# The causal mask of grouped attention, added by VectorE in PSUM instead of by three TensorE products per head

## The reference

```
q = q * cos + rotate_half(q) * sin          # 32 heads, 512 tokens, 128 wide
k = k * cos + rotate_half(k) * sin          # 8 heads, each used by 4 query heads
scores = q @ k.T / sqrt(128)
scores = scores * scale                     # keys 0..34 by 0.5, keys 35..106 by 1.5, for queries from 107 on
scores = scores + where(qpos >= kpos, 0, float32 min)
attn = softmax(scores) @ v
out = attn @ wo.T
```

## Time and profile before

| | |
|---|---|
| median of 3 runs | 3147.85 us (3145.69 to 3154.63) |
| the profiled execution, its own time | 3139.91 us |
| its span, first to last instruction | 3137.8 us |
| mean granted TensorE clock | 0.874 |
| busy in the whole span | PE 2461.8 us (78%), DVE 2008.0 (64%), ACT 1584.7 (51%), POOL 1127.0 (36%) |
| first and last mask product | 1760.9 and 2550.0 us |

### The profile page before, as it was taken

One profiled execution on the slowest core, in us unless ns is written; L12 is line 12 of the kernel. 1 busy time (PEld: TensorE's weight loads), 2 busy tenths in 40 slices (PEclk: granted clock), 3 DMA queues, 4 the chain that ended last, 5 costly groups with the idle time before them and its releaser, 6 DMA issues.

```text
span 3137.8 us, 36611 instructions
## 1 busy us (share of the span) xinstructions
PE 2461.8 (78%) x12408; PEld 1933.7 (62%) x12408; DVE 2008.0 (64%) x3083; ACT 1584.7 (51%) x3186; POOL 1127.0 (36%) x992
## 2 busy tenths in 40 slices
PE   6986989578688857868799799998999986951076
PEld 4344357467577746756678688876788864841065
DVE  4824744688677667867653567772677754398974
ACT  1632631465665256666520466662666641699511
POOL 2011046141122441112267456565465640300180
PEclk8886899689898968989999899999999997965588
DMA  6132122110200120010023111122111110100010
GB/s 212 42 97 80 42 78 81 48 38 4 64 21 24 44 71 21 18 51 21 28 70 110 43 44 45 48 58 61 31 53 48 52 41 14 54 14 0 0 48 27
DMA packets 85967, 152.56 MB, mean 49 GB/s; under 512 B 8632, under 2 KB 17464, under 8 KB 85656
## 3 DMA queue, kind: packets, MB, share of 16 engines
q1 hardware_dynamic: 85784, 150.24, 16.3%
HBM read 135.06 MB, written 14.75 MB: 48 GB/s over the span
## 4 chain that ended last, share of the span: by engine, by line
PE 37%; ACT 8%; DVE 5%; issue 4%; POOL 3%; POOLq 0%; ACTq 0%; DVEq 0%
PE ps L614 33%; ACT tables L1274 5%; PE ps L628 4%; POOL w_lo L558 1%; ACT m L1156 1%; ACT tables L1128 1%; POOL w_hi L557 1%; POOL k L571 1%; DVE stat L1328 1%; DVE n L1336 0%; DVE tables L1748 0%; DVE f_lo L1313 0%; DVE x_sb L1316 0%; DVE f_hi L1312 0%; ACT m L1138 0%
## 5 line engine op out<-in xcount | busy, mean ns | idle before, releaser
L557 POOL TENSOR_SCALAR w_hi<-w_in 128x512 fp32r<-128x512 f32 x418 | 315.1, 754 | 1453.3 <-PE ps L614 886.9
L558 POOL TENSOR_TENSOR w_lo<-w_in,w_hi 128x512 fp32r<-128x512 f32 x418 | 596.5, 1427 | 34.9
L614 PE MATMUL ps<-hT_hi,w_lo 128*128 128x512 f32 x864 | 353.8, 409 | 19.2 <-DVE a L1358 12.9
L1517 DVE TENSOR_TENSOR_SCAN m<-m,m 128x1028 f32<-128x1028 f32 x128 | 307.3, 2400 | 67.2 <-ACT m L1156 59.7
L628 PE MATMUL ps<-tables,m 128*128 128x128 f32 x1024 | 187.8, 313 | 202.5 <-ACT tables L1128 117.9
L614 PE MATMUL ps<-hT_hi,w_hi 128*128 128x512 f32 x864 | 341.7, 396 | 0.0
L614 PE MATMUL ps<-hT_lo,w_hi 128*128 128x512 f32 x864 | 341.7, 395 | 0.0
L614 PE MATMUL ps<-m,tables 128*128 128x128 f32 (+1 forms) x2112 | 323.1, 302 | 13.3 <-ACT tables L1128 12.6
L614 PEld LDWEIGHTS ps<-m,tables 128*128 128x128 f32 (+1 forms) x2112 | 293.2, 213 | 23.4 <-ACT tables L1128 17.2
L628 PEld LDWEIGHTS ps<-tables,m 128*128 128x128 f32 x1024 | 129.7, 158 | 238.3 <-ACT tables L1128 141.3
L1128 ACT ACTIVATE tables<-ps 128x512 f32<-128x512 f32 x256 | 151.0, 590 | 184.5 <-PE ps L628 183.0
(11 more groups left out here) (232 smaller groups left out, 5503.0 us busy)
## 6 DMA issues: line engine op xcount, KB each, us to landing
w_in<-units SPq DMA_DIRECT2D x418, 256.0 KB, 2.6
stack_scratch<-a SPq DMA_DIRECT2D x48, 256.0 KB
a<-stack_scratch SPq DMA_DIRECT2D x64, 192.0 KB, 4.5
m<-bc_scratch SPq DMA_DIRECT2D x16, 512.0 KB, 5.2
out<-x_sb SPq DMA_DIRECT2D x2, 1024.0 KB, 4.3
tables<-small SPq DMA_DIRECT2D x1, 1399.0 KB, 10.1
x_sb<-x SPq DMA_DIRECT2D x4, 256.0 KB, 3.5
x_sb<-x SPq DMA_DIRECT2D x1, 1024.0 KB, 7.2
```

The source lines that it names most:

```text
L557: c["did"](nc.gpsimd.tensor_scalar(w_hi[:, r], raw, 1.0, 1.0, ALU.mult, ALU.mult), s["unit_hi"])
L558: c["did"](nc.gpsimd.tensor_tensor(w_lo[:, r], raw, w_hi[:, r].bitcast(F32), ALU.subtract), s["unit_split"])
L614: ins = T.matmul(out, lhsT, rhs, start=start, stop=stop)
L1517: V.tensor_tensor_scan(states, m_dA[:, dA:dA + NG].rearrange("p a t -> p (a t)"), states, 0.0, ALU.mult, ALU.add)\
```

## The change

The float32r copies `ident_r` and `mask_r` and the two DVE instructions that made them are gone. The scores of row tiles 1 to 3 end with the third product of `mm3`, which now raises `g_scores`. A new DVE helper `hide(t)` adds the mask to the diagonal block of row tile t in place: it reads PSUM and the table in SBUF and writes PSUM. `maxima_1` calls it for tile 1, `maxima_2` for tiles 2 and 3 before their row maxima.

```
-        ident_r = sb("ident_r", [P, P], F32R)
-        mask_r = sb("mask_r", [P, P], F32R)
...
-                            mm3(o, q_hi, q_lo, g_k_hi[:, g, 0:w], g_k_lo[:, g, 0:w], True, False)
-
-                            mm(o[:, t * P:w], ident_r[:, :], mask_r[:, :], False, True, s["g_scores"])
+                            mm3(o, q_hi, q_lo, g_k_hi[:, g, 0:w], g_k_lo[:, g, 0:w], True, True, s["g_scores"])
...
-                        go(V.tensor_copy(ident_r[:, :], ident))
-                        go(V.tensor_copy(mask_r[:, :], col("mask")))
...
+                def hide(t):
+
+                    bank, at_s = g_bank[t]
+                    own_keys = ps[:, bank, at_s + t * P:at_s + (t + 1) * P]
+                    return V.tensor_tensor(own_keys, own_keys, col("mask"), ALU.add)
+
...
                 def maxima_1():
 
                     need(s["g_scores"])
+                    go(hide(1))
+                    did(V.tensor_tensor(g_s0, ps[:, 0, 0:P], col("key_scale"), ALU.mult))
                     go(top(1))
-                    did(V.tensor_tensor(g_s0, ps[:, 0, 0:P], col("key_scale"), ALU.mult))
                     did(V.tensor_tensor(g_s0, g_s0, col("mask"), ALU.add))
...
                     need(s["g_scores"])
+                    go(hide(2))
+                    need(s["g_scores"])
+                    did(hide(3))
                     go(top(2))
-                    need(s["g_scores"])
                     did(top(3))
```

More of the change, by code:

```diff
@@ L1358, in attn_qk @@
                         go(V.tensor_tensor(a_lo[:, qk], ps[:, 4 + qk], a_hi[:, qk].bitcast(F32), ALU.subtract), s["a_lo"])
-                    if b == 0 and m == 0:
-                        go(V.tensor_copy(ident_r[:, :], ident))
-                        go(V.tensor_copy(mask_r[:, :], col("mask")))
                     if b == 0 and m == 1:
```

## The result

| | before | change |
|---|---|---|
| median of 5 runs | 3145.69 us (3142.61 to 3154.63) | 3124.86 us (3116.91 to 3128.16) |
| ratio to before, 95% interval | | 0.9932 [0.9911, 0.9953] |
| the profiled execution, its own time | 3139.91 us | 3127.87 us |
| its span | 3137.8 us | 3126.0 us |

The change is faster, by 20.8 us between the medians. The two profiled executions differ by 12.0 us. Whole executions scatter by about as much as the change is worth, so what it does in its own stage is measured there: from one fixed product of PE to another, in the traces.

A forecast was written before the change was run, and what follows sets the result against it. PE was taken to bound the grouped attention. Per batch, -0.20 (head 0), +0.53 (head 1) and +8.41 (heads 2 to 31), doubled, gave 17.5 us off 3147.85: 3130.3 us; own range 3124 to 3136, 8 in 10 within 3122 to 3144.

The forecast's parts named there:

- The bound: Grouped attention: PE busy for all 46.86 us of a four-head group, so time off its list shortens the span.
- What leaves PE: Scores of each head: three mask products removed, worth 0.29 us per head by steps from start to start.
- The rival of the bare steps: Scores on PE: only the mask products' own steps go, 0.18 us per head, 3136.8 us; chance 0.12.
- the estimate of 15.6 us made from its 81 ns: PE's scores: 192 removed products priced at the skill page's sustained step of a 128-column product with weight load.
- What comes to DVE: `maxima_1` and `maxima_2`: three additions per head at 0.28 us each, making DVE 0.70 us later per head.
- The rival with additions as dear as L1611: DVE's additions each cost 0.29 us more, using up the room at the query split: 3133.2 us; chance 0.12.
- Is there room for it?: DVE's turn with `add(3)`: 4.48 us of work fits in 4.49; POOL's query split keeps 0.69 us to spare.
- The edges: Start and end of each batch: head 0 loses 0.20 us, head 1 gains 0.53, heads 2 to 31 gain 8.41.
- In the last head ... I charge nothing there: Last head of each batch: DVE's shifts lie ahead of ACT's copies of transposed tiles, so no loss is counted.
- DVE becomes the bound: Query split after a key split: DVE's lateness makes groups slower once additions pass 0.90 us each; chance 0.06.
- the gain is given back elsewhere: PE's wait moves to ACT's swap or the weight units; time stays within 0.3% of 3147.85 us; chance 0.06.

The follow-up runs named there:

- e2: Kernel before with the DVE mask additions put on top, PE's mask products kept: group of four heads 46.86 us, stage 1.8 us longer than before.
- e1: Changed kernel without the three DVE additions, row tiles 1 to 3 left unmasked: median 3130.09 us, stage 16.5 us shorter than before.
- e5: Changed kernel with row tile 0's scores kept in PSUM, so its mask addition has one SBUF input: median 3126.83 us.
- e6: Changed kernel with row tile 0 in PSUM and each mask addition covering two row tiles, two per head instead of four: median 3127.7 us.
- e3: Changed kernel with each of the three DVE additions made twice: median 3143.97 us, stage 3.6 us longer than before.
- e4: Changed kernel with the two float32r tiles of mask and identity still allocated and made once by DVE: ratio 0.9931 to the kernel before.
- e9: Changed kernel, unaltered, measured and profiled again on another chip: ratio 0.995 [0.9938, 0.9963] to the kernel before.

## Why the prediction was right, and where it was not

**The bound.** Right. PE was busy for all of 46.86 us and is busy for all of 45.71 (the forecast said 45.7), and e2 shows that DVE's additions alone leave the group at 46.86.

**What leaves PE.** Right at 0.29 us per head, and right in where it comes from. Set beside each other, the scores of one head before and in the change draw apart by 0.06 at each removed product and by another 0.05 to 0.06 at each of the two long steps of 0.23 and 0.29 that followed one (0.18 and 0.23 in their place); 0.24 ahead of the transposes stayed. The rival of the bare steps, 0.18 per head, would have made the group 46.14 us; the bank still changes at those places, so it was not the bank. That the weight load behind a short product is what made the steps long is a reading that no run tests. The page "TensorE: Matmul & The Clock Gate" ("Back-to-back issue gap") of the Trainium skill, by the estimate of 15.6 us made from its 81 ns, does not agree: the 26 distances per batch outside the edges shrank by 0.29 us each in the mean, 97 ns per removed product. (The 3132.3 us made from it also left out the edges' 0.4, which the rival of the bare steps counts.)

**What comes to DVE.** Right: 0.293 us per addition where 0.28 was taken. The unknown, a write into PSUM, cost 12 ns. The page "SBUF — State Buffer" ("Who interferes with whom") of the Trainium skill, by which one SBUF input does not contend with GpSimd, agrees: 192 additions with one SBUF input lasted 279 to 300 ns, also with PSUM as output, while L1611 with two reached 1417. The rival with additions as dear as L1611 falls.

**"Is there room for it?"** This step failed in size. It left 0.69 us to spare at the split of the query; 0.05 to 0.50 was measured, and 0.05 is none. The instructions I added were counted well (0.73 against 0.70), but three things around them were not. The 0.98 it started from was one turn's: the same kernel had 0.79 and 0.63 at two others. L1611 was taken at 0.29 from one row, though the rows' mean was 573 ns, and in its new place it was held for 0.30 more. And one of GpSimd's own instructions, L555 ahead of L556 and the split, lasts 1.14 to 1.15 us in every such turn, where it lasted 0.94 in most before:

```profile
1950.89 0.94 POOL L557 TENSOR_SCALAR w_hi<-w_in 128x512 fp32r<-128x512 f32 x1
```

The runs tell the last two apart. In e1, without the additions, L555 lasts 0.94 and the room is 0.71 to 0.73 in nine of the ten turns, close to the 0.69 forecast; in the tenth L555 lasts 1.14 and the room is 0.52. In e5, with the additions but without L1611's second SBUF input, L555 lasts 1.14 and the room is 0.49 to 0.51 everywhere. So the longer L555 takes 0.20, and L1611's holds take up to 0.45 more and make the spread. What lengthens L555 is a reading: DVE's L1544, which has two SBUF inputs, runs beside it in the change (from 1945.52, L555 from 1945.55). (The 3.78 us counted as work in the earlier trace rows also held 0.15 us of waiting for a transposed tile. It is gone in the change, but the instruction behind that copy starts 0.12 later, so the count came out.)

**The edges.** This is the term of the sum that was mis-sized. In the window from the first to the last scores the forecast is 17.2 us (17.5 less the last head), measured 13.6. By the differences from head to head, batch 0 and batch 1: head 28 was taken as unchanged and lost 0.45 and 0.46; head 30 was taken as a full gain and lost 0.45 and 0.45, 0.74 short each; head 2 gained nothing for 0.29; head 1 gained 0.31 and lost 0.16 for a forecast gain of 0.53, but that head differs by 0.75 between profiles of one kernel, so its share says nothing. Head 0 was taken 0.20 too dear: it stayed at 14.80. Together 3.5 of the 3.6. Less head 1 in both, the forecast is 16.1 and 13.5 was measured.

At head 28 VectorE's additions are the cause: without them (e1) it is 9.99, as before. At head 30 they are a part. Of the 0.74 short, leaving the additions out gives back 0.30 in batch 0 and 0.23 in batch 1 (e1, 8.91 in batch 0), taking L1611's second SBUF input away gives back 0.40 (e5, 8.81), and both remedies on VectorE together 0.47 (e6, 8.74). The last 0.27 came back in no run. In the trace of the change DVE goes from `add(3)` (2100.30) to that copy (2103.13) without a pause, and the scores begin only at 2100.39; so shorter scores on PE do not bring the copy forward. "In the last head ... I charge nothing there" held, but I did not look at the head before it, where PE's copy wait lay uncovered at 0.31 us already.

**DVE becomes the bound.** Not here, but nearer than forecast. The rival put the point at 0.90 us per addition; e3, where a doubled addition with its waits comes to about 0.5 (0.73 us per head as above, and about 0.8 for the second round, over three; 0.6 with the 0.26 by which the mask of tile 0 got longer), already gave the whole gain back. It did so for the most part through ACT's swap and scaling, which is the mechanism of the rival "the gain is given back elsewhere", and only for 0.10 of 0.77 through the query's split.

**The size of the whole.** 3124.86 us was measured where 3130.3 was forecast, 20.8 us less than before instead of 17.5, while the stage gave 13.9 with its last head. That the total came nearer to the forecast than the stage did is luck: e4 finds nothing outside the stage, e9 gave 17.0 us between the medians for the same kernel, and the start of the stage moves by 5 us and the stretch behind it by 3.5 us between profiles of the same kernel. 13.9 of 3143 us is a ratio of 0.9956; it lies within the second interval and just above the first's end of 0.9953. What makes whole executions scatter stays open beyond the granted clock of their first stages, and what decides that clock does too.

## What to carry to other kernels

Where one engine is busy for all of a repeated group, work taken from it is worth its step from start to start, including how it lengthens the next instruction's step, and that is to be read from neighbours and not from its duration. An engine that takes the work over with a quarter of its time idle is not free of charge: look for its fullest turn and for the turns at the start and end of the stage where the other's cover is missing, and take durations there from the spread of a row and not from one lucky instance. When whole executions scatter by as much as the change is worth, measure the distance between two fixed instructions around the stage, profile one kernel more than once, and set the part aside that does not repeat. And when an instruction seems to be just in time in every turn, compare with a turn where it is known to be late: the same 0.05 us stood in both.

## What the runs showed of the hardware

A VectorE addition of 128x128 in place in PSUM lasts 290 ns (the median of 192), one over two pieces of 128 columns 422 to 433 ns, in one bank or in two, so merging two saves about 0.15 us and a wait. A VectorE instruction with two SBUF inputs beside a busy GpSimd lasted 281 to 1417 ns for the same work, and each of its rows over 300 ns overlapped a GpSimd instruction; the same with one input in PSUM lasted 289 to 290 in all 64 cases. A TensorE product of 128 columns that stepped by 60 ns was worth 97 ns when it was taken out, since the step behind it got shorter too. One program began the same stage 24 us later than another after equal instruction lists, with a granted clock of 0.72 against 0.94 between 100 and 200 us.
